# A four-layer network on one core: products that nobody reads, put behind each phase of the delta rule

## The reference

```python
# first attention: B, L, D, H = 2, 512, 128, 4 per call, chunks
q, k, v, kb = l2norm(q), l2norm(k), v * beta, k * beta
A = where(tri, 0, -kb @ k.T)
for i in range(1, chunk):
    A[i, :i] += A[i, :] @ A[:, :i]
inv = A + eye                      # inverse of a unit triangular matrix
u, w = inv @ v, inv @ kb
def step(S, (q, k, u, w)):         # over the chunks, in order
    attn = where(strict, 0, q @ k.T)
    u_adj = u - w @ S
    out = q @ S + attn @ u_adj
    S = S + k.T @ u_adj
# third attention: the same rule with a decay exp(g) on S at each step, 64 columns a head
```

## Time and profile before

| | |
|---|---|
| median of three runs | 5786.07 us (5783.81 to 5801.77) |
| span of the profiled execution, first to last instruction | 5785.5 us |
| mean granted clock of TensorE | 0.754 |
| TensorE busy | 4147.9 us, 72% |
| VectorE busy | 2997.7 us, 52% |
| ScalarE busy | 1935.9 us, 33% |
| GpSimd busy | 817.3 us, 14% |

### The profile page before, as it was taken

The page is one execution under the profiler, slowest core; times in us unless marked ns, Lnnn a source line. Parts: engine busy times, 40 slices in busy tenths (PEclk is TensorE's granted clock), DMA queues, the critical chain, the costliest instruction groups (busy, mean ns, idle before and its releaser), DMA issues.

```text
span 5785.5 us, 94866 instructions
## 1 busy us (share of the span) xinstructions
PE 4147.9 (72%) x39740; PEld 3210.4 (55%) x39740; DVE 2997.7 (52%) x7965; ACT 1935.9 (33%) x4236; POOL 817.3 (14%) x600
## 2 busy tenths in 40 slices
PE   6786969367787878873747767586777777776298
PEld 5675849255565555552636556474445555445277
DVE  4445352525545454557355555546666666665232
ACT  2233231223333333330232332424444554552122
POOL 0000000231110011101600000002111111110434
PEclk7555555588888898885756665667889898898599
DMA  9200000140000000001210000000000000000255
GB/s 261 51 1 1 2 1 2 55 158 1 1 1 1 1 1 1 1 1 36 29 41 2 1 1 2 0 2 2 1 1 1 1 1 1 1 1 17 70 158 142
DMA packets 140860, 152.33 MB, mean 26 GB/s; under 512 B 7808, under 2 KB 128002, under 8 KB 139792
## 3 DMA queue, kind: packets, MB, share of 16 engines
q1 hardware_dynamic: 119024, 128.21, 7.6%
q0 software_dynamic: 21408, 18.05, 1.8%
HBM read 87.38 MB, written 59.76 MB: 25 GB/s over the span
## 4 chain that ended last, share of the span: by engine, by line
PE 50%; DVE 29%; ACT 12%; issue 3%; POOL 2%; DMA 2%; another core or an unknown queue 1%; SPq 0%; DVEq 0%; POOLq 0%; ACTq 0%
PE banks_lane L801 4%; ACT work L3231 4%; PE banks_lane L422 3%; PE banks_lane L3668 2%; PE banks_lane L1885 2%; PE banks_lane L1251 2%; PE banks_lane L809 2%; PE banks_lane L3117 2%; PE banks_lane L3152 1%; PE banks_lane L950 1%; PE banks_lane L3139 1%; ACT work L1979 1%; PE banks_lane L3097 1%; DVE work L2793 1%
## 5 line engine op out<-in xcount | busy, mean ns | idle before, releaser
L422 PE MATMUL banks_lane<-constants,work 128*128 128x128 f32 x968 | 203.3, 360 | 495.8 <-DVE work L408 209.6
L422 PEld LDWEIGHTS banks_lane<-constants,work 128*128 128x128 f32 x968 | 154.6, 186 | 566.1 <-DVE work L408 197.5
L402 POOL TENSOR_TENSOR weights<-weights,constants 128x4 f32<-128x4 f32 x76 | 78.5, 1033 | 2032.1 <-DVE weights L397 2032.1
L422 PE MATMUL banks_lane<-constants,weights 128*128 128x128 f32 x596 | 125.8, 348 | 332.7 <-DVE weights L408 93.3
L3231 ACT ACTIVATE work<-banks_lane,weights 128x192 f32<-128x192 f32 (+1 forms) x512 | 249.0, 505 | 136.2 <-DVE weights L3328 136.1
L422 PEld LDWEIGHTS banks_lane<-constants,weights 128*128 128x128 f32 x596 | 89.2, 179 | 362.6 <-issue 166.5
L402 POOL TENSOR_TENSOR work<-work,constants 128x4 f32<-128x4 f32 x76 | 77.3, 1018 | 1200.0 <-DVE work L397 1200.0
L3335 POOL TENSOR_TENSOR weights<-weights,constants 128x16 f32<-128x16 f32 x64 | 185.4, 2896 | 377.8 <-DVE weights L3243 377.8
L3324 DVE TENSOR_REDUCE weights<-banks_lane 128x2 f32<-128x384 f32 (+1 forms) x256 | 122.5, 520 | 145.6 <-PE banks_lane L3139 145.6
L3152 PE MATMUL banks_lane<-constants,work 128*128 128x128 f32 x896 | 137.0, 299 | 80.2 <-DVE work L3316 42.7
L2032 DVE TENSOR_REDUCE work<-banks_lane 128x2 f32<-128x512 f32 x256 | 158.9, 685 | 68.1 <-PE banks_lane L1899 67.4
(11 more groups left out here) (779 smaller groups left out, 11121.1 us busy)
## 6 DMA issues: line engine op xcount, KB each, us to landing
work<-experts_dram_l_ffn SPq DMA_DIRECT2D x39, 964.0 KB
room_l_ffn<-work SPq DMA_DIRECT2D x30, 1188.0 KB, 15.0
work<-experts_dram_l_ffn SPq DMA_DIRECT2D x23, 512.0 KB
weights<-weights_dram SPq DMA_DIRECT2D x1, 4833.5 KB, 14.1
work<-room_l_ffn SPq DMA_DIRECT2D x36, 132.0 KB
weights<-weights_dram SPq DMA_DIRECT2D x1, 4112.0 KB, 12.8
weights<-bands_dram SPq DMA_DIRECT2D x1, 4096.0 KB, 13.2
weights<-room_l_ffn SPq DMA_DIRECT2D x26, 132.0 KB
```

The costliest lines, as they stand in the source:

```text
L402: pool.tensor_tensor(n.rstd, n.rstd, c("neghalf", cols=(0, n.rstd.shape[1])), ALU.pow).then_inc(*u.pool.step(name))
L422: done = pe.transpose(bank[0:rows, t * P:(t + 1) * P], block, c("ident"))
```

## The change

A helper `keep_busy` issues n products of the identity with the first columns of `masks("later")`, into a place in PSUM. Nothing reads the place; no semaphore counts them. It is called behind the signalling product of a phase: three of 256 columns after each left and right step of levels 1 to 4, four after left 5, right 5 and left 6, three after the values and three after the outputs of each chunk, and eight of 512 columns ahead of the transposes of the keys. In the third attention the last gets a wait for the copy of the first value rows, whose bank it writes. The 512-column group stands once a unit, and each unit has 24 groups of three and six of four in its two pairs, so that both attentions together issue 384 groups of three, 96 of four and 16 of eight.

```diff
+def keep_busy(pe, masks, place, n):
+
+    for _ in range(n):
+        pe.matmul(place, masks("ident"), masks("later")[:, 0:place.shape[1]], start=True, stop=True)
...
+FILL_SMALL, FILL_JOIN, FILL_VALUES, FILL_ENTRY = 3, 4, 3, 8
...
             made.then_inc(*u.pe.step(f"left{pair}_{n}"))
             next(between, None)
+            keep_busy(pe, self.masks, b[0][:, 0:BANK // 2], FILL_SMALL)
             yield f"left{pair}_{n}"
...
             made.then_inc(*u.pe.step(f"right{pair}_{n}"))
             next(between, None)
+            keep_busy(pe, self.masks, b[0][:, 0:BANK // 2], FILL_SMALL)
             yield f"right{pair}_{n}"
...
         made.then_inc(*u.pe.step(f"left{pair}_5"))
         next(between, None)
+        keep_busy(pe, self.masks, b[0][:, 0:BANK // 2], FILL_JOIN)
         yield f"left{pair}_5"
...
         pe.matmul(b[3][:, :], w("fuse_hidden"), m.zT).then_inc(*u.pe.step("held"))
+        keep_busy(pe, run_masks, b[0][:, :], FILL_ENTRY)
         pe.wait_ge(*u.dve.at("ready"))
...
                 pe.matmul(b[2][:, 0:P], m.kbq[:, chunk, 1, :], d.S, start=True, stop=False)
+                keep_busy(pe, run_masks, b[0][:, 0:BANK // 2], FILL_VALUES)
                 yield f"u{chunk}"
...
                 made.then_inc(*u.pe.step(f"out{chunk}"))
+                keep_busy(pe, run_masks, b[0][:, 0:BANK // 2], FILL_VALUES)
                 yield f"out{chunk}"
...
         yield "rows"
+        pe.wait_ge(*u.act.at("v_rows0"))
+        keep_busy(pe, run_masks, b[0][:, :], FILL_ENTRY)
         pe.wait_ge(*u.dve.at("ready"))
```

More of the change, by code:

```diff
@@ L1025, in __init__ @@
                       for lane in range(LANES)]
+        for m in self.lanes:
+            m.delta.masks = run.masks
         self.units, self.filters, self.products = units_of(run, ["l0_attn"]), None, None
@@ L1056, in pe @@
     def pe(self, pe, u):
-        m, b, w, c = self.lanes[u.lane], u.banks, self.w, self.c
+        m, b, w, c, run_masks = self.lanes[u.lane], u.banks, self.w, self.c, self.run.masks
         d = m.delta
@@ L2667, in pe @@
                 pe.matmul(b[2][:, 0:d.width], m.kbq[:, chunk, 1, :], d.S).then_inc(*u.pe.step(f"carried{chunk}"))
+                keep_busy(pe, run_masks, b[3][:, 0:BANK // 2], FILL_VALUES)
                 yield f"u{chunk}"
@@ L2675, in pe @@
                 made.then_inc(*u.pe.step(f"out{chunk}"))
+                keep_busy(pe, run_masks, b[1][:, 0:BANK // 2], FILL_VALUES)
                 yield f"out{chunk}"
```

## The result

| | before | after |
|---|---|---|
| median, runs taken beside each other | 5793.92 us (4 runs, 5783.81 to 5801.78) | 6092.46 us (4 runs, 6076.72 to 6100.95) |
| ratio, 95% interval | | 1.0519 (1.0500 to 1.0539) |
| span of the profiled execution | 5785.5 us | 6099.6 us |
| mean granted clock | 0.754 | 0.747 |

The changed kernel is slower by 298.5 us on the medians and by 314.1 on the two profiled spans; the forecast was +350 on the span, 6135 us, with 6010 to 6210 as the range.

What follows compares the result with a forecast made beforehand. TensorE at 1.2 GHz was taken as the bound in both attentions. Added products cost 369 us gross, less 23 hidden, plus 4 for entry: +350 on the 5785.5 us span, about 6135 us, range 6010 to 6210.

Steps and rivals of the forecast that it cites:

- The clock stays at 0.50: In the delta-rule levels of both attentions, the added products leave TensorE's clock at 0.50.
- the nearest row: First attention's state steps: 42% wide products at clock 0.50, so levels with 30% wide products were taken at 0.50 too.
- nothing carries it into the stretch where TensorE is full: At a half's start, first phases wait for VectorE, so a clock raised by entry products would not last into the levels.
- the open end named in the last sentence of the forecast: The forecast would be wrong above all if the clock answered to something in the added products that no row held.
- The price: Each added 256-column product costs 0.213 us at 0.50, plus net 0.16 us of tile change per group among small tiles.
- The sum: Both attentions: 369 us gross, less 23 hidden, plus 4 for entry, gives +350 us.
- entry, -1 us a pass: First attention: entry products hidden by a wait, and transposes behind them at 1.00 save 1 us a pass.
- What is hidden: Groups standing before waits for other engines are free: 2.4 us a pass in first attention, 3.2 in third, 23 in all.
- C: Idle time elsewhere in the attention stretches absorbs more of the added products: 6074, or 6018 without tile-change costs; chance 0.10.
- B: Clock rises only in the first attention's state and output products, saving 20 us a pass: about 6053; chance 0.11.
- A: In both attentions the clock rises to 2.4 GHz and stays: -192, about 5600 us; chance 0.06.
- D: Nothing measurable, if TensorE had slack for 369 us, where it has 85; chance 0.02.

Runs made afterwards that it cites:

- The run with three products behind a large start: Kernel with large first groups, three products instead of four behind left and right steps of levels 3 and 4 in the second half and third attention: 5722.11 us.
- the double groups: Changed kernel with six, eight and six products in its groups instead of three, four and three, entry as it was: 5921.24 us in a single run.
- The run with 16 columns: Changed kernel with all groups in place, but each product 16 columns wide instead of 256 or 512: 5912.83 us, ratio 1.0217.
- The run with the entry groups alone: Changed kernel with only the eight 512-column products ahead of the keys' transposes, all other groups left out: 5795.51 us, ratio 1.0003.
- four in each: Kernel with large first groups, but four products in every level group of the first attention's second half and the third attention: 6029.50 us, ratio 1.0455.
- the first attention's first half alone: Kernel with large first groups, cut to six in that half's level and join groups plus its entry group, nothing anywhere else: 5742.32 us, ratio 0.9923.
- large first groups: Changed kernel with 8 or 12, then 6, then 4 products by level; six throughout first attention's first half; fewer value groups, no third-attention entry: 5704.66 us.

## Why the prediction held, point by point

**The clock stays at 0.50: right for the change, with a reason that does not carry.** The windows show it, and the clock line. The argument went by the nearest row: levels with 30% wide products lie below the state steps with 42%, which get 0.50, so they get 0.50. The run with three products behind a large start has the same mixture in levels 3 and 4 at 1.00, and the double groups reach it with another. What decides is not the mixture alone but the mixture and the level at which it begins: groups of four give 69 us or 91 us for the same half. The change comes into the first attention's first half at 1.00, as forecast, but has fallen by 84 us; in the others it begins at 0.50, and three in a group do not raise it. That "nothing carries it into the stretch where TensorE is full" was true, and it is the step on which the outcome hung; that something could carry it was the open end named in the last sentence of the forecast.

**The price: right.** 0.80 was forecast for a group of three among the small tiles (3 x 0.213 + 0.16); 0.795 was measured in the second half's levels, 0.75 where the filter's products stand ahead. The run with 16 columns shows that 0.22 of it is not columns.

**The sum: 36 us too large, and 54 too large in the two attentions** (148 + 148 against 177 + 173). The stages without the products, which the forecast left as they were, grew by 17 us and go the other way: that the total came out nearer than its parts is luck. (The forecast's own terms give 44 and 43 us a pass, not the 46 and 41 of its last paragraph; measured were 36 to 38 and 34 to 41.) 36 of the 54 stand in the first halves, 22 in the first attention and 14 in the third: 17.3 us was measured in pass 2 of the first attention where 23.9 - 0.5 - 1.0 = 22.4 were forecast. The start of that half, in the kernel before and in the changed one (TensorE in order of time, pass 2), shows which term was off.

```profile
338.92 2.12 PE L782 MATMUL banks_lane<-work 32*128 32x256 f32 x16 [1.48 <-ACT work L1184]
...
349.82 1.92 PE L801 MATMUL banks_lane<-weights,work 64*64 64x32 f32 x32
```

```profile
374.11 1.17 PE L791 MATMUL banks_lane<-work 32*128 32x256 f32 x16 [1.58 <-ACT work L1203]
...
377.07 0.50 PE L429 MATMUL banks_lane<-masks 128*128 128x256 bf16 x3
378.12 0.73 PE L819 MATMUL banks_lane<-weights,work 32*32 32x16 f32 x64 [0.55 <-DVE work L913]
...
380.12 1.72 PE L810 MATMUL banks_lane<-work 64*64 64x32 f32 x32
...
383.92 1.92 PE L810 MATMUL banks_lane<-weights,work 64*64 64x32 f32 x32
```

The second lane's score starts 11.3 us behind the half's first score before (327.6 us) and 10.1 after it in the changed kernel (364.0), and the fourth level step 22.2 us (349.82) and 19.9 us (383.92). With three groups in between, the stretch got 2.3 us shorter, where 3 x 0.80 - 0.47 - 1 = 0.9 more were forecast: 3.2 of the 5.1 us. The entry products put the transposes, the second lane's score and the first two steps at 1.00, which the forecast sized at 1 us from the first pass alone, where those steps are at 1.00 already; in pass 2 the score takes 2.12 us before and 1.17 after. The run with the entry groups alone shows the same by itself: 94.0 to 94.4 us for 97.2. So the term "entry, -1 us a pass" was mis-sized, with about -3 measured in passes 2 to 4, and the first groups, at 1.00, cost less than 0.80 each. The other 1.9 us are small differences behind this stretch: the level and join groups took 0.75 and 0.97 us each where 0.80 and 1.01 were forecast, and the value groups 4.0 us together instead of 5.1. No single term makes up the 54 us.

**What is hidden.** The two groups that were to vanish in the third attention's waits do: the second lane's first level step stands 18.5 us behind the half's first score in both kernels (2998.8 to 3017.29, 3161.4 to 3179.92). Behind it the half grew by 17.8 us (14.3 in the pass that was longer before) where 20.6 was forecast; the second halves by 16 to 23 for 22.6 with the entry, and in the first attention by 20 to 21 for 21.9.

**The rivals.** C (more is hidden, 6074) lies nearer to the span's 6099.6 than the forecast's 6135, but not by what it stood for: in the third attention's levels just the two groups vanish that were counted, and what was too large are prices and the entry's effect. B (only the first attention's state and output products rise) did not happen, 163 to 181 us is at 0.50. A (the clock rises) did not happen with the change's numbers, but its mechanism is real: with the counts moved to the halves' beginnings it gives 5704.66 us, short of the 5600 that was worked out for it, since one half in pass 1 and one in the third attention stay out and the other first halves there hardly get shorter at 0.9 of the clock (61.12 of 68.8 us busy there; waits for VectorE take most of the rest). D did not happen.

**Busy and the clock.** In the changed kernel TensorE is busy 76.00 of 76 us at 0.50. The Trainium skill, TensorE: Matmul & The Clock Gate, section "Why this matters for your kernels", has it that a TensorE kept continuously busy gets its full rate; these 76 us do not agree, although the profile shows no gap in them.

## What to carry to other kernels

Work that is put into the queue of an engine that is always busy costs its own time, so products meant to raise a clock must be judged by whether they raise it: read the granted clock half by half and pass by pass, not the mean (0.754 and 0.747 stand for kernels 299 us apart). Here the level fed itself: the same four products a phase, and in two levels the same three, ran at 1.00 or at 0.50, by what stood ahead of them. Large groups at the beginning of a stretch with smaller ones behind them gave 1.1 to 1.4% on the kernel before, six in every group of one half alone gave 0.8%, and filler that doesn't change the level is only paid for. Before that, see whether another engine bounds the stretch once TensorE is faster.

## What the runs showed that was not expected

Short pauses of TensorE inside the levels ("issue": it waits for nothing that the profile shows) go together with the loss of a whole half. Pauses of 1.03, 1.08, 1.18 and 1.39 us in the third attention, 2.17 and 2.23 us at 93 us in the kernels with doubled groups and with four in each, and 0.66 us at 103.18 stand ahead of a fall of the clock that follows within 2.1 us, and one of 1.60 us, up to 87.84 in the kernel with the first attention's first half alone, has the fall inside it; seven others, of 0.57 to 0.82 us, had 16 us or more at 1.00 behind them. But the clock also falls without one. In the kernel with four in each group, pass 4 of the first attention (93.8 us for 77.8), it fell at 930 us, with TensorE at work all the time and six products in each group:

```profile
929.69 0.97 PE L429 MATMUL banks_lane<-masks 128*128 128x256 bf16 x6
930.59 1.97 PE L859 MATMUL banks_lane<-weights 64*64 64x64 f32 x16
```

Pass 1 of the first attention fell back in every kernel with six or more, at 79 to 105 us, with the same code at 79, 88 and 94 us in different kernels; what sets it apart stays open. Where the clock falls, the same groups keep it down for the rest of the half (14 and 16 us in second halves of the third attention, 36 to 50 us in pass 1 of the first). Falls in some executions and not in others would explain why the kernels that reach 1.00 spread more from run to run (57 us for the one with large first groups, 127 for the one with the first half alone, whose slowest execution has a mean clock of 0.76 where the others have 0.78, against 12 for the kernel before beside them); but only one execution of each was profiled, and no pause was put in or taken out to try it. Nor is it shown what makes the pauses.

That the wide four-byte products lose their clock with two-byte products of 16 columns in all the places (86.4 to 86.7 us for 75.1 in the third attention's first half, in three passes of four) was not expected either; why one pass kept it stays open.
